# The last round of a token attention: ranks and places of the third last chunk in the middle of the second half

## The reference, cut to what matters

```
x = conv_attention(x)                        # 16 images of 128 x 16 x 16, softmax over the images
t = tokens(x)                                # 16 images of 256 tokens of 128
t = t + compositional_attention(layernorm(t))   # 8 searches, 2 retrievals, width 16, then w_out
z = layernorm(t)
logits = z @ Wg                              # 8 experts
best two experts of each token, softmax of their two logits
t = t + sum over the two experts of  weight * (silu(z @ W1[e]) @ W2[e])
```

## Time and profile before

| | |
|---|---|
| median of 3 runs | 814.94 us (809.99 to 817.6) |
| the profiled execution | 813.52 us, of it span 811.8 us |
| PE busy | 670.3 us (83%) |
| DVE busy | 443.0 us (55%) |
| ACT busy | 309.9 us (38%) |
| POOL busy | 241.2 us (30%) |
| round 7, second half, on PE | from 546.65 to 561.34 us |
| experts' first tile arrives | 602.6 us |

### The profile page before, as it was taken

How to read it: one execution, slowest core, us unless ns; L and a number is a source line. 1 busy time by engine, 2 the same in 40 slices (tenths; PEclk the granted TensorE clock), 3 DMA queues, 4 the chain that set the end, 5 groups by cost and what they waited for, 6 DMA issues and landing times. The chain is left out here.

```text
span 811.8 us, 11835 instructions
## 1 busy us (share of the span) xinstructions
PE 670.3 (83%) x3761; PEld 556.1 (69%) x3761; DVE 443.0 (55%) x1216; ACT 309.9 (38%) x616; POOL 241.2 (30%) x280
## 2 busy tenths in 40 slices
PE   5999999992878999989899897977329999889840
PEld 4888888871657988878888796966217666666630
DVE  5233343335565868676768586664306565555635
ACT  5111011110534545443434353432117676566720
POOL 2100662002900000131403122223631644545470
PEclk9999999995888999999989898887559999999975
DMA  9999771000044122131222204000155566666518
GB/s 331 324 354 355 244 247 52 0 0 0 1 130 130 52 80 89 43 115 43 95 63 80 78 21 137 11 18 18 37 157 190 170 213 183 201 197 200 192 35 310
DMA packets 56372, 105.42 MB, mean 130 GB/s; under 512 B 8872, under 2 KB 21817, under 8 KB 56192
## 3 DMA queue, kind: packets, MB, share of 16 engines
q1 hardware_dynamic: 51328, 96.24, 36.5%
q0 software_dynamic: 4992, 8.54, 3.0%
HBM read 58.15 MB, written 48.42 MB: 131 GB/s over the span
## 5 line engine op out<-in xcount | busy, mean ns | idle before, releaser
L1320 PE MATMUL bank<-rvx,s_expd 128*128 128x96 f32 x1024 | 140.7, 285 | 11.3 <-issue 5.6
L1320 PEld LDWEIGHTS bank<-rvx,s_expd 128*128 128x128 f32 x1024 | 133.9, 203 | 14.3 <-ACT s_expd L825 7.3
L1580 POOL DMA_INDIRECT y_slots<-virt,pad_l x92 | 93.2, 1013 | 100.2 <-DVE virt L1631 77.4
L825 ACT ACTIVATE s_expd<-bank 128x512 f32<-128x512 f32 x128 | 75.7, 598 | 115.2 <-PE bank L1304 100.4
L996 DVE TENSOR_REDUCE s_max<-bank 128x2 f32<-128x512 f32 x128 | 87.6, 688 | 56.9 <-PE bank L1283 44.1
L53 PE MATMUL bank<-pad_h,w_h 128*128 (+1 forms) x216 | 88.2, 408 | 8.5 <-DVE pad_l L322 8.5
L53 PE MATMUL bank<-k_stack,pad_h 128*128 128x512 f32 x184 | 81.7, 444 | 14.4 <-issue 8.1
L744 POOL DMA_INDIRECT x_slots<-rows,slot_of x64 | 62.9, 983 | 78.6 <-DVE rows L1124 61.3
L54 PE MATMUL bank<-pad_l,w_h 128*128 (+1 forms) x216 | 85.8, 397 | 0.0
L55 PE MATMUL bank<-pad_h,w_l 128*128 (+1 forms) x216 | 85.6, 397 | 0.0
L713 POOL TENSOR_TENSOR ln_rstd<-ln_var,power 128x4 f32<-128x4 f32 x16 | 16.4, 1023 | 198.6 <-DVE ln_var L972 198.6
(11 more groups left out here) (232 smaller groups left out, 1123.1 us busy)
## 6 DMA issues: line engine op xcount, KB each, us to landing
pad_h<-w_split SPq DMA_DIRECT2D x46, 512.0 KB
x_slots<-blank SPq DMA_DIRECT2D x8, 2112.0 KB, 20.4
qk_rows<-qk SPq DMA_DIRECT2D x16, 512.0 KB
k_stack<-qk_rows SPq DMA_DIRECT2D x96, 64.0 KB, 2.2
q_stack<-qk_rows SPq DMA_DIRECT2D x48, 128.0 KB, 2.4
pad_l<-x_slots SPq DMA_DIRECT2D x23, 264.0 KB
e_raw<-in_w SPq DMA_DIRECT2D x16, 256.0 KB, 3.5
w_split<-e_high SPq DMA_DIRECT2D x16, 256.0 KB, 2.6
```

The costliest lines, as they stand in the source:

```text
L825: nc.scalar.activation(expd[:, s % 2].rearrange("p a i -> p (a i)"), ps_st[s % 2][:, :], ACT.Exp).then_inc(exp_done, 1)
L1320: last = pe.matmul(ps_pv[s // 4][:, at:at + RVW], expd[:, s % 2, a, i * P:(i + 1) * P], rvx[:, ring, 2 * b + a, :], start=(a == 0), stop=( ...
L1580: pool.indirect_dma_start(out=y_slots[:, :], out_offset=bass.IndirectOffsetOnAxis(ap=ids, axis=0), in_=y_rows[:, t % 2, j, :], in_offset=N ...
```

## The change

In the last round only, three steps of chunk 5 (the third last) are moved. `share_exp(5)` goes on ACT from behind the fifth exponential of the second half to behind the first. `rank(5)` goes on PE from step 6 of the second half to step 2, behind the turn back of chunk 6. `place(5)` goes on VectorE from step 7 to step 3, which puts it ahead of the second and third parts of `retrieve(7, 0)`. Nothing is added or removed, and GpSimd's program is the same.

```
             for s in range(S):                      # ACT, second half
                 exponent(g, 1, s)
...
+                if s == 0 and stage == LAST:
+                    share_exp(g - 2)
...
-                    if s == 4 and g >= 2:
+                    if s == 4 and g >= 2 and stage != LAST:
                         share_exp(g - 2)
...
                 if s == 5:                          # VectorE, second half
                     retrieve(g, 0, 2)
-                if g >= 2 and s == 7:
+                if g >= 2 and s == (3 if stage == LAST else 7):
                     place(g - 2, ring)
...
                     if s == 2:                      # PE, second half
                         tail_turn_back(g - 1, 1 - ring)
+                        if stage == LAST:
+                            rank(g - 2)
...
-                if g >= 2 and s == 6:
+                if g >= 2 and s == 6 and stage != LAST:
                     rank(g - 2)
```

## The result

The changed kernel took **820.49 us** (median of 20 runs, 816.79 to 825.52) beside 815.03 for the kernel before (20 runs, 805.71 to 820.1): a ratio of **1.008**, interval 1.0056 to 1.0104. That is 5.5 us slower, where 2.5 us faster was forecast. The profiled execution took 819.84 us, with a span of 818.1.

The account below looks back on a forecast made before the run. The prediction took the serial tail after GpSimd's late inverse root of chunk 7 (576.11) as the bound outside PE's limit. Root 2.5 us earlier: 814.94 - 2.5 = 812.4 us, chance 0.65, range 807.5 to 817.1.

Parts of the forecast that it names:

- share_exp(5): On ACT in round 7's second half: a short activation of 0.2 us, covered because PE is still in the first product.
- rank(5): Five small matmuls on PE at step 2, 0.26 us at half clock; ranks ready at about 553.15.
- place(5): On VectorE from 553.15 to 554.15; delays retrieve(7, 0)'s later parts to about 556.1, at no cost.
- The queue: GpSimd's transfers of chunk 5 begin at 554.95 instead of 561.03, 6.1 us early; queue free at 565.0.
- route(6): On VectorE: starts with its logits at 557.8 to 558.1, takes 3.25 us, ends at 561.05 to 561.35.
- the rival by the clock: PE's clock stays at 1.2 GHz for steps after rank(5); 2.2 us slower, 817.1; chance 0.08.
- The rival by the lock: GpSimd held out wholly while VectorE works; root at 578.1, 2.0 us slower, 816.9; chance 0.02.
- the transfers themselves: Chunk 5's issues beside more VectorE work: 0.1 us each, 0.8 in all, against 2.2 us of slack; sum stays.
- the term of the last product: PE's last product of round 7, ending at 561.34, moves by 0 to 0.13 us; taken as 0.
- retrieve(7, 1): On VectorE: waits for the copy ending at 561.78, starts at 561.81 instead of 563.38, 1.57 us early.
- the forecast's sum: GpSimd's inverse root of chunk 7 starts at 573.62 instead of 576.11, bound by data: 2.5 us gained, bounds 0.9 to 3.1.
- a rival in the prediction (0.10): Chunk 5's issues wait for something else, or the experts' loop takes the gain back; 814.9; chance 0.10.

Follow-up runs that it names:

- late8: Changed kernel with chunk 5's eight transfers held behind round 7's last product; 815.83 us, ratio 1.0024 to the kernel before.
- half4: Changed kernel with four of chunk 5's transfers early, the other four behind round 7's last product; 815.02 us, ratio 1.0003 to the kernel before.
- probe_kind: Kernel before, chunk 1 sent by plain transfers, chunk 2 by indirect ones of 32 rows; first halves of rounds 3 to 7: 26.7, 22.8, 27.5, 23.6, 22.1 us.
- probe_count: Kernel before, chunks 0 to 4 with 8, 4, 2, 8 spaced, no transfers; first halves of rounds 3 to 7: 26.6, 22.8, 22.8, 19.0, 17.0 us.
- pace1: Kernel before with one cleared tile on GpSimd between the transfers of chunks 0 to 4; 789.42 us, ratio 0.9669 to the kernel before.
- before_b: Kernel before, unaltered, run again on a fourth chip, where no signals were held; 787.2 us.
- late8_b: Changed kernel with chunk 5's eight transfers behind the last product, on the fourth chip; 788.24 us, ratio 1.0026 to the kernel before there.

## Why the prediction was wrong

**Step by step, what held.** *share_exp(5)* and *rank(5)*: covered; ranks ready at 553.2 (forecast 553.15). *place(5)*: idle before it 4.17 us, done at 554.2 (554.15). *The queue*: first issue 555.00 (554.95), eighth ends 564.90 (565.0). *route(6)*: from 558.05 (557.8 to 558.1). The clock: unchanged, so the rival by the clock is refuted. The rival by the lock: eight issues took 0.96 to 1.04 us each beside VectorE's work, so it is refuted too.

**The step that failed** is the one on the transfers themselves: "Chunk 5's issues now lie beside more work of VectorE. ... so 0.1 us for each of eight, 0.8 in all, against 2.2 us of slack (565.0 to 567.27). The sum stays." With it fell the term of the last product, which was to move by 0 to 0.13 us from 561.34 and ended at 566.05. The transfers were moved from behind PE's last step into PE's last steps, and I priced what that does to GpSimd's issues and not what it does to PE's signals. In the profiled execution it is 3.9 us of PE standing still for the last scores' signal (559.56 to 563.65), 0.8 for the last product, which stands alone and at a clock that falls (1.73 us, where the second half of the joined pair took 0.95), and 0.5 for that product's own signal (566.05 to 566.61, less the usual 0.02). ACT's copy is 5.25 us behind its forecast, and with 0.1 more before VectorE starts, `retrieve(7, 1)` and the root are 5.4 behind theirs (578.98 against 573.62). With that term the sum at the root is -2.5 + 5.4 = +2.9, which is what the traces show (576.11 to 578.98). late8 and half4 show the term by taking it away; probe_kind, probe_count and pace1 show that it takes indirect transfers in quick succession.

They are not enough by themselves. In the kernel before twelve lie 1.27 us apart from 561.03 to 576.09, behind the second half, where PE gives a signal only every few us: all that the trace keeps of them from 561 to 602 rise within 0.01 us.

The forecast could have had it. Each of rounds 3 to 7 had such transfers beside its first half; rounds 3 to 5, with the same work as round 2 (22.8 and 22.9 us in before_b), took 3.8 to 5.5 us longer than it and had waits released by `remote`. I read only round 7's second half, the one place without them, and carried its lengths over to a stage in which they would lie. The rival that ended slower was to be this one, at about 5 us, and not the two that I took from rules.

The Trainium skill ("SBUF — State Buffer", "Who interferes with whom") has PE and ACT never waiting on anyone, and GpSimd's transfers as the ones that VectorE can hold up. The section speaks of access to SBUF, and as far as PE's matmuls go the trace agrees: beside the transfers scores took 0.48 us and products 1.03, as in the kernel before. Read as a rule for a stage's time it would have no wait here; but what waits for PE was held up to 5 us beside GpSimd's transfers, so for that the measurement decides against it.

**Where nothing holds the signals, the forecast's sum was right**: 2.38 us at the root against 2.5, `retrieve(7, 1)` 1.48 us earlier (539.13 to 537.65) against 1.57, released by ACT's copy. Of the whole, 0.9 and 1.1 us show (0.9989 and 0.9986), with intervals that reach from 2.5 and 2.8 us faster to 0.9 and 0.6 slower, so that a gain of the whole is not shown.

**What stays open.** The held signals account for the 2.9 us at the root, and the median lost 5.5, with an interval of 4.6 to 8.5: about half of the loss is not accounted for. With late8 it is the same: 4.7 us less, of which 1.7 are at the root (577.31). At the experts' first turn the loss of the profiled executions is 2.25 us and in the whole 6.3; the rest is the experts' part, 213.2 us long instead of 209.2. The kernels with the old order have 207.6, 207.7, 209.2, 210.3 and 211.7 there, those with the new one 208.3 to 214.3 (ten traces). These overlap, but their means lie 1.9 us apart (209.3 and 211.2), and late8_b, with its root 0.7 us earlier than before_b, is 1.0 us slower as a whole. So either it is the scatter of executions, or the experts' loop gives back some 1 to 2 us of what the tail wins; that was a rival in the prediction (0.10), no run here separates the two, and I have no mechanism for the second. PE's signals are also late in the experts' part on the chips that hold them, by up to 1.6 us, but in the changed kernel no more often than in the one before: 12 and 13 of them by over 0.1 us.

Not tried either is what holds the signals, and why only in some groups of runs: each chip has one group of runs, so that the chip is not told apart from something else that differed between the groups. One rival touches all of the times here. The traces with held signals have also lost records of signals. In the kernel before they keep 5,843 of the 7,872 that its transfers raise, and 24 of the 128 of chunk 0's; before_b keeps 7,835, and 127. In probe_kind, chunk 1, sent plain, has all of its 128, and chunk 2, sent indirectly, 21. So it is beside the transfers that hold signals that most records are lost, and it may be the recording of signals that holds PE back. Each execution here has a span and a granted clock on record, so none is known to have run without recording, and this is open. Lost records do not hold a signal by themselves: pace1 kept 51 of chunk 0's 128, and no signal of PE was late beside them.

## What to carry to other kernels

Before you move transfers into a stage, look at a stage of the same kernel that already has such transfers beside it, and compare its length with one that has none; waits released by `remote` are a mark, though not each held signal leaves one. Transfers that are issued early are not free for the others: bring them forward only as fast as they are needed, as a little distance (1.8 us in place of 1.27) gave 25 us of 815 where signals are held, and cost nothing that shows where they are not (1.0006). And time a small gain on more than one chip: this change lost 5.5 us on one, and on two others there is no such loss, and perhaps a gain of about 1.

## What was not expected of the hardware

- Eight indirect transfers from GpSimd, issued 1.27 us apart, can hold back the signals of PE, by up to 6 us and until 1.7 us after the last issue's end; not those of ACT, VectorE or GpSimd (0.13 us at most). The same at 1.16 us with 32 rows each. Not so four at 1.27 us (probe_count's chunk 1; with chunk 5's first four, half4, a hole of 1.08 us was left), eight at 1.8 us or more, eight plain ones in 4.41 us, or twelve at 1.27 us where PE's signals are few. Whether they are held without the recording was not measured.
- It differs by chip, or by something that went with the chip: the same kernel before took 815.03, 815.62 and 815.25 us in three groups of runs, 787.19 and 787.23 in two others. In the profiled executions of before and before_b the granted clock is 0.905 and 0.919, and PE is idle for 142 and 129 us. With one cleared tile between transfers the kernel takes 789.42 on one of the former and 787.57 on one of the latter, so the spacing does away with nearly all of that difference.
